# First layer's sampled attention in sixteen turns, with the coverage test in PSUM and merged value products

## The reference, cut to what matters

```python
K, V, Qp = k @ Wk.T + bk, v @ Wv.T + bv, q @ Wq.T + bq         # first layer: 16 heads of 16
loc_x = mod(ref + (Qp @ Woff.T + boff) + loc, sign_lens)       # 5 sampling points per query and head
sk, sv = 0.5 * (w0 * K[i0] + w1 * K[i1]), 0.5 * (w0 * V[i0] + w1 * V[i1])   # linear between neighbours
attn = softmax(sum_d(Qh / sqrt(16) * sk)); ctx = sum_k(attn * sv); out = ctx @ Wo.T + bo
# layers 1 to 3: dense attention; in 2 and 3 K, V have biases bk, bv, and out = ctx @ Wo + bo
```

## Time and profile before

| what | value |
|---|---|
| three runs | 1224.21, 1225.88, 1226.24 us; median 1225.88 us |
| profiled execution | 1230.04 us; its span 1228.2 us, so 1.84 us lie around the span |
| busy share of the span | PE 88%, DVE 65%, ACT 40%, POOL 18% |
| mean granted TensorE clock | 0.91 of full |
| DMA | 121.84 MB, mean 99 GB/s |

### The profile page before, as it was taken

One profiled execution on the slowest core, in us unless ns is written; L12 is line 12 of the kernel. 1 busy time (PEld: TensorE's weight loads), 2 busy tenths in 40 slices (PEclk: granted clock), 3 DMA queues, 4 the chain that ended last, 5 costly groups with the idle time before them and its releaser, 6 DMA issues.

```text
span 1228.2 us, 17469 instructions
## 1 busy us (share of the span) xinstructions
PE 1079.4 (88%) x6632; PEld 626.1 (51%) x6632; DVE 801.3 (65%) x1433; ACT 488.2 (40%) x712; POOL 221.7 (18%) x264
## 2 busy tenths in 40 slices
PE   8598994899998886998799999889789999699898
PEld 4245552344443443997344444444578787244445
DVE  4978948688978813354578886971644654689716
ACT  2453221066766650111016775664312221057552
POOL 3563811211111002000501110100400400211000
PEclk9798896789999996999869999999999999679899
DMA  5686820201331052794151231200244240100001
GB/s 187 217 250 208 296 84 1 84 21 39 122 101 38 11 156 72 263 371 157 41 162 41 60 87 50 55 6 14 91 156 151 88 149 27 29 7 16 1 27 35
DMA packets 78571, 121.84 MB, mean 99 GB/s; under 512 B 9888, under 2 KB 52036, under 8 KB 78478
## 3 DMA queue, kind: packets, MB, share of 16 engines
q1 hardware_dynamic: 58778, 79.41, 21.0%
q10 hardware_dynamic: 18932, 39.10, 9.1%
q0 software_dynamic: 768, 2.10, 0.5%
HBM read 92.45 MB, written 27.81 MB: 98 GB/s over the span
## 4 chain that ended last, share of the span: by engine, by line
PE 61%; DVE 23%; issue 4%; ACT 3%; DMA 2%; POOL 2%; ACTq 0%; SPq 0%; DVEq 0%; POOLq 0%
DVE arena L1955 13%; PE bank L1373 11%; PE bank L1333 11%; PE bank L1544 10%; PE st_bank L1472 3%; PE bank L1484 3%; PE st_bank L1358 3%; PE st_bank L1241 2%; DVE xn L1655 2%; PE st_bank L1544 2%; PE bank L1403 1%; PE st_bank L1301 1%; PE bank L1339 1%; PE bank L1182 1%; PE st_bank L1249 1%
## 5 line engine op out<-in xcount | busy, mean ns | idle before, releaser
L1955 DVE TENSOR_REDUCE arena<-bank 128x1 f32<-128x512 f32 x640 | 400.2, 683 | 70.8 <-PE bank L1333 70.7
L1056 ACT ACTIVATE arena<-st_bank 128x1024 f32<-128x1024 f32 x320 | 316.1, 1022 | 159.2 <-PE st_bank L1358 157.8
L1333 PE MATMUL bank<-g_a 64*128 64x512 f32 x480 | 184.9, 517 | 13.4 <-DVE arena L1955 3.3
L1373 PE MATMUL bank<-arena,vaug 128*9 128x256 f32 (+2 forms) x2560 | 177.0, 396 | 1.8 <-ACT arena L1056 1.8
L1333 PEld LDWEIGHTS bank<-g_a 64*128 64x128 f32 x480 | 75.7, 199 | 122.9 <-DVE arena L1955 83.8
L1544 PE MATMUL bank<-g_a,g_w 128*128 128x512 f32 x512 | 117.6, 390 | 4.3 <-DVE g_w L2157 3.2
L1358 PE MATMUL st_bank<-g_a 64*128 64x512 f32 x480 | 117.7, 445 | 0.0
L1544 PEld LDWEIGHTS bank<-g_a,g_w 128*128 128x128 f32 x512 | 95.8, 188 | 25.4 <-DVE g_w L2157 3.6
L1373 PEld LDWEIGHTS bank<-arena,vaug 128*9 128x9 f32 (+2 forms) x2560 | 56.8, 93 | 81.5 <-issue 44.4
L1333 PE MATMUL bank<-g_x,g_a 64*128 64x512 f32 x160 | 64.2, 528 | 9.9 <-DVE arena L1955 3.2
L837 POOL CAST arena<-arena 8x128 fp32r<-8x128 f32 x40 | 11.2, 280 | 315.4 <-ACT arena L1049 315.4
(11 more groups left out here) (284 smaller groups left out, 1506.0 us busy)
## 6 DMA issues: line engine op xcount, KB each, us to landing
arena<-in_glu_w SPq DMA_DIRECT2D x39, 512.0 KB, 3.3
arena<-kv_table SPq DMA_DIRECT2D x16, 1024.0 KB, 7.1
ctxT<-in_glu_w ACTq DMA_DIRECT2D x22, 512.0 KB, 6.5
arena<-in_w SPq DMA_DIRECT2D x20, 512.0 KB, 6.3
kparts<-arena ACTq DMA_DIRECT2D x12, 512.0 KB, 3.9
arena<-in_w ACTq DMA_DIRECT2D x12, 512.0 KB, 3.5
g_a<-kparts SPq DMA_DIRECT2D x24, 192.0 KB
kv_table<-arena ACTq DMA_DIRECT2D x16, 256.0 KB, 2.1
```

The source lines that it names most:

```text
L1056: act.activation(prob[sl % PROBS], st_bank[sl % 2][:], ACT.Exp, scale=scale).then_inc(exp_ready, 1)
L1333: pe.matmul(bank[TURN_BANKS[place % 3]], Qc[gi % KQ_BUFS][rows, hh, qt * P:(qt + 1) * P], Kc[gi % KQ_BUFS][rows, half * CH:(half + 1) * CH ...
L1373: ins = pe.matmul(bank[7][at:at + dh + 1, 0:D], vaug[l][:, b * KT + 2 * m + i, h0 + hh, :], tiles[:, a], start=(m == 0 and i == 0), stop=( ...
L1955: dve.tensor_reduce(mxh[gi % 2][:, col, hf:hf + 1], bank[TURN_BANKS[place % 3]], AX.X, ALU.max).then_inc(max_red, 1)
```

## The change

The two loops over tiles on DVE and POOL become one loop of 16 turns, a product each. The softmax is done by batch inside the turns: the maximum of a batch in turn 4 or 8, its subtraction, exponential and sum in the next, its scaling in the one after; the weighing by the attention of tile t stands in turn t + 6, so that turns 6 to 8 weigh for both kinds of product. POOL's product n waits for the weighing of turn n - 1. The weighing by the attention has a buffer of its own (`a_tmpv`). `rest` is called by a list (`RESTS`): none in turns 0 to 3, one each in 4 to 10, two in 11 to 13, three in 14.

The coverage test works by batch on halves of 320 elements, in PSUM banks 2 and 3, with a help array in SBUF; two tiles of the table go ahead of it. Its sum is taken by PE after ten of the sixteen table products, in bank 0, and the flag is made after turn 2. DVE then reads two flags and runs turns 3 to 15 in one of two copies, with or without the general path:

```diff
+            kv0_rows(KV_FIRST, KV_FIRST + KV_BY_DVE)
+            for b in range(B):
+                ins = dve.tensor_scalar(inside[b], points[b], float(M // 2 - BACK), float(-M), ALU.is_ge, ALU.mult)
...
+            def turn(n, uncovered):
+                if n in (QT + 1, NT + 1):
+                    b = n // NT
+                    dve.tensor_tensor(sc[:, rows_b[b]], sc[:, rows_b[b]], each_sample(a_mx, b), ALU.subtract).then_inc(sub0_ready, 1)
+                if n in (QT + 2, NT + 2):
+                    b = n // NT
+                    ch.link(dve.scalar_tensor_tensor(sc[:, rows_b[b]], sc[:, rows_b[b]], 0.5, each_sample(a_sm, b), ALU.mult, ALU.mult))
+                weighed = n - QT - 2
+                if 0 <= weighed < NT:
+                    last = weigh(weighed)
+                if 1 <= n <= NT:
+                    last = weigh_scores(n - 1)
...
+                elif 1 <= n < 2 * NT - 2:
+                    last.then_inc(prod_used, 1)
+                dve.wait_ge(prod_ready, n + 1)
...
+                if n < len(RESTS):
+                    for k in range(sum(RESTS[:n]), sum(RESTS[:n + 1])):
                         rest(k)
...
+            with dve.If(all_covered):
+                for n in range(FLAG_AT + 1, 2 * NT):
+                    turn(n, False)
...
+            with dve.If(some_uncovered):
+                for n in range(FLAG_AT + 1, 2 * NT):
+                    turn(n, True)
+                dve.wait_ge(ctxn_ready, NT)
+                general(1, range(NT), more_context)
+            dve.wait_ge(ctxn_ready, NT)
             dve.sem_inc(ctxn_ready, NT)
```

On PE the key products go round four banks, and the three value products of a chunk become one of 416 columns without bias products. ACT's three value copies now read that one bank. The value biases of layers 2 and 3 go into the output bias instead: bo + bv @ Wo, made by PE after the gate logits and copied by ACT; PE's ranking comes behind these products:

```diff
+                if k >= 4:
+                    pe.wait_ge(prepk_lo, k - 3)
...
+                for i in range(DC):
+                    ins = pe.matmul(bank[QT_BANKS[k % 4]][:, 0:VW], ctxT[:, i, k * P:(k + 1) * P], a_wv[:, i, :], start=(i == 0), stop=(i == DC - 1))
...
+            for l in (2, 3):
+                o = bank[5][0:1, (l - 2) * D:(l - 1) * D]
+                for c in range(EC[l]):
+                    pe.matmul(o, w[l]["bv"][:, c:c + 1], w[l]["o"][:, c, :], start=(c == 0), stop=False)
+                ins = pe.matmul(o, onesf[0:1, 0:1], w[l]["bo"][:], start=False, stop=True)
+            ins.then_inc(prepv_mm, 1)
             pe.wait_ge(onehot_ready, 1)
```

ACT's order changes with it: row weights 4 to 6 go between the last table copies, weights 7 behind the first chunk, and the two exponentials behind chunks 1 and 5. SP has two more small loads (the value biases) among the late ones, reads the flag ahead of all value windows, and has three skips of the general path in place of two:

```diff
-            for t in range(NWIN):
-                window_load(NT + t, t, 1)
             sp.wait_ge(flag_ready, 1)
...
+            general_windows(0, range(QT))
+            for t in range(QT):
                 window_load(NT + t, t, 1)
-            general_windows(1, NT)
+            general_windows(0, range(QT, NT))
+            for t in range(QT, NT):
+                window_load(NT + t, t, 1)
+            general_windows(1, range(NT))
```

More of the change, by code:

```diff
@@ L109 @@
 KCHUNKS = PREP0[4]
+PREP_BANKS = (2, 3, 4, 5)
+VW = sum(EW.values())
+V0 = {l: sum(EW[i] for i in range(1, l)) for l in ATT}
+RESTS = [0] * 4 + [1] * 7 + [2] * 3 + [3]
+assert sum(RESTS) == KCHUNKS
+KV_BY_DVE = 2
+FLAG_AT = 2
 QT_BANKS = (0, 1, 6, 7)
@@ L424, in build @@
         a_W = r2.take([NT, HK, WIN])
-        a_S = [r2.take([WIN, H0]) for _ in range(2)]
+        a_S = [r2.take([WIN, H0]) for _ in range(3)]
         r3 = Region(w0kv_at)
         a_A = [r3.take([H0, WIN]) for _ in range(3)]
+        a_tmpv = r3.take([HK, WIN])
+        assert r3.at <= w0q_at
         a_tmp = Region(w0q_at).take([HK, WIN])
@@ L940, in _ @@
             row_weights(1)
-            for n in range(KV_FIRST, 2 * KV_FIRST, 2):
-                kv0_store(n)
-                kv0_store(n + 1)
-                if n < 2 * KV_FIRST - 2:
-                    row_weights((n - KV_FIRST) // 2 + 2)
-            for n in range(2 * KV_FIRST, NCT):
-                kv0_copy(n)
-                if n > 2 * KV_FIRST:
-                    kv0_store(n - 1)
-            kv0_store(NCT - 1)
+            for i in range(3):
+                kv0_store(KV_FIRST + 2 * i)
+                kv0_store(KV_FIRST + 2 * i + 1)
+                if i < 2:
+                    row_weights(2 + i)
+            kv0_copy(12)
+            row_weights(4)
+            kv0_copy(13)
+            kv0_store(12)
+            kv0_copy(14)
+            kv0_store(13)
+            row_weights(5)
+            kv0_copy(15)
+            kv0_store(14)
+            row_weights(6)
+            kv0_store(15)
             act.wait_ge(ld_small, 16 * 4)
@@ L1242, in _ @@
                 ins.then_inc(prepk_mm, 1)
[L1243 to L1252 removed]
+                if k >= 4:
+                    pe.wait_ge(prepv_evac, k - 3)
@@ L1745, in rest @@
                 dve.wait_ge(prepk_hi, k + 1)
-                src, (hi, lo) = bank[2 + k % 2][0:n, :], (a_parts[k % PBUFS][0:n, i] for i in range(PARTS))
+                src, (hi, lo) = bank[PREP_BANKS[k % 4]][0:n, :], (a_parts[k % PBUFS][0:n, i] for i in range(PARTS))
                 if l == 1:
@@ new lines, in _ @@
+            kv0_rows(KV_FIRST, KV_FIRST + KV_BY_DVE)
+            for b in range(B):
+                ins = dve.tensor_scalar(inside[b], points[b], float(M // 2 - BACK), float(-M), ALU.is_ge, ALU.mult)
+            ch.link(ins)
+            for b in range(B):
+                ins = dve.scalar_tensor_tensor(points[b], points[b], float(BACK), inside[b], ALU.add, ALU.add)
+            ch.link(ins)
+            for b in range(B):
+                ins = dve.tensor_scalar(inside[b], points[b], 0.0, None, ALU.is_ge)
@@ new lines, in _ @@
+            for n in range(FLAG_AT + 1):
+                turn(n, None)
+            dve.wait_ge(sum_mm, 2)
+            dve.tensor_scalar(flag_i[:, 0:1], bank[0][0:1, 0:1], float(P * NT * HK) - 0.5, None, ALU.is_lt)
+            dve.tensor_scalar(flag_i[:, 1:2], bank[0][0:1, 0:1], float(P * NT * HK) - 0.5, None, ALU.is_ge).then_inc(flag_ready, 1)
+            dve.wait_ge(flag_ready, 1)
+            some_uncovered, all_covered = (dve.value_load(flag_i[0:1, i:i + 1], min_val=0, max_val=1) for i in range(2))
```

307 lines of the change are left out of this document (146 added, 161 removed).

## The result

The changed kernel takes 1194.55 us in the median of four runs (1193.10 to 1195.89) against 1225.05 for the kernel before beside it: ratio 0.9752, 95% interval 0.9732 to 0.9771. The profiled execution took 1195.89 us, span 1193.4, mean clock 0.914.

What follows compares the result with a forecast made beforehand. POOL's sixteen products were the longest chain, their idle time on the path through the key preparation. Transposes 23.3 us sooner, 1.5 gained, 3 and 2.2 lost: -19.6 from 1230.04, adjusted to the median, gave 1206 us, range 1196 to 1217.

Steps and rivals of the forecast that it cites:

- Start, turns 2 to 7, softmax: DVE and POOL, start to product 8: product 2 at 50.1 us (9.2 gained), product 7 at 82.5, softmax inside the turns.
- First value window: SP's late loads and skip delay the first window: it lands at 91.6 us, product 8 at 92, 3 late (0 to 6).
- Key preparation: Last four turns: turn 14 waits for stores and for PE partly at half clock, 6 us (0 to 14).
- The rival that I gave 0.18: DMA transfers take over between 74 and 137 us: windows and stores 6 to 8 us late, 1213 us; chance 0.18.
- The skip: DVE's branch over the general copy after the last value sum: 2.5 us (1 to 4) on the path.
- Behind the stage: After the transposes begin: 1.5 us gained on ACT's context copy, 3 lost to PE's half clock (0 to 6).
- The bias products: Second layer, five products between logits and ranking: 5 to 5.5 us, making the ranking 2.2 us later (0 to 3).
- The sum: Whole kernel: -23.3 - 1.5 + 3 + 2.2 = -19.6 us, predicting 1206 us.
- everything fits: Whole stage: chunks keep up, PE stays warm, first window in time, transposes at 143 or sooner, 1197 us; chance 0.15.
- the rival that ended slower: PE's key preparation at half clock takes over the stage: transposes at about 183 us, time 1242; chance 0.06.

Runs made afterwards that it cites:

- the run with the windows first: Changed kernel with SP's fifteen late loads behind all eight value windows instead of ahead of the first; ratio 0.9802 to the kernel before, stage 102.2 us.
- at the old price: Changed kernel with a key chunk's value products by layer again, eight instead of two; ratio 0.978 to the kernel before, stage 103.9 us.
- the twelve loads out of the way: Changed kernel, value windows ahead of late loads, twelve loads issued after the last sum; ratio 0.9760 to the kernel before, 0.9765 with stores also issued sooner.
- The run with the skip behind the sum: Changed kernel with DVE waiting for the last value sum inside the covered branch, before the skip; ratio 0.9785 to the kernel before, stage 104.7 us.
- the run with the test alone: Kernel before with only the new coverage test (in PSUM, by batch, its halves around the first table tiles); ratio 0.994 to the kernel before.

## Why the prediction was wrong, step by step

The forecast's times, counted from product 0 (38.92 before), beside three profiles of the changed kernel:

| us after product 0 | forecast | first | second | third |
|---|---|---|---|---|
| product 2 | 11.2 | 12.0 | 12.5 | 12.5 |
| product 5 | 28.4 | 28.7 | 28.9 | 28.9 |
| product 6 | 36.1 | 35.1 | 35.4 | 35.4 |
| product 7 | 43.6 | 42.2 | 42.5 | 42.5 |
| product 8 | 53.1 | 52.4 | 54.8 | 57.1 |
| product 11 | 72.5 | 71.0 | 72.0 | 74.1 |
| product 15 | 93.6 | 92.0 | 92.3 | 94.0 |
| last sum issued | 103.7 | 98.3 | 98.9 | 101.1 |
| transposes | 108.4 | 101.6 | 102.3 | 103.8 |

**Start, turns 2 to 7, softmax: right.** Every product up to product 15 stands within 1.6 us of its forecast in the first profile. The coverage test was priced at 0.5 an instruction and took 0.45. Its reason was half right: not PSUM alone, but also which instructions stand beside a product, and which kind they are.

**First value window: right in place, open in size.** 5.6 us of gap against "some 5" in the first profile; 10 in the third. SP's late loads set it, as the run with the windows first showed. While the window was late, the softmax by batch was worth only 0 to 2 us.

**Key preparation: the step that failed.** I put its tail at 6 us (0 to 14). Product 15's sum was issued 2.4, 2.7 and 3.2 us after the product, so the tail is 2.4 to 3.2. The mechanism was there, DVE waiting for ACT in turns 13 and 14 and ACT for stores, but I added PE at half clock to it, and PE was ahead. In the first profile its granted clock was 1.00 from 105 to 135 us, its chunk took 3.11 us, the pairs overlapping (3.43 for the last four), not 3.55, and at the old price it lengthened the stage by only 2. What the tail hangs on is the transfers. The pages' DMA issues, first of before and then of after, give the stores of 512 KB that ACT waits for 3.9 and 5.8 us to landing:

```profile
kparts<-arena ACTq DMA_DIRECT2D x12, 512.0 KB, 3.9
...
kparts<-arena ACTq DMA_DIRECT2D x12, 512.0 KB, 5.8
```

The rival that I gave 0.18 has its mechanism shown, and its sign too: four of the eight value windows landed after 9 us or more in the first profile, none before. Its price (6 to 8 us) is not shown. In the changed kernel the tail costs the 2.4 to 3.2, and with the windows sooner, the stores sooner and the twelve loads out of the way the whole stage is 4 to 6 us shorter still.

**The skip: mis-sized.** 2.5 us forecast, 0.4 to 1.1 measured. I read 2.15 and 3.05 as a price to be added; but here a skip runs from the issue of the instruction ahead of it (2.4 to 3.9 us from there in all these kernels), and a 2.27 us sum now stands there. The Trainium skill's page Runtime: NRT & Kernel Launch (Instruction fetch mechanics) says that a taken branch to a target outside the fetched pages waits until that page is fetched. The run with the skip behind the sum agrees, with 3.89 us of waiting and nothing beside it; the fetch itself no run shows.

**Behind the stage: nearly right.** I forecast 1.5 lost between the transposes and the attention behind them (3 for the clock, 1.5 gained on ACT). From the first transpose to the first attention product it took 60.3 us before and 62.3, 61.1 and 61.2 after: 0.8 to 2.0. In the two kernels in which TensorE was busy up to the transposes and kept the full clock it took 58.1 and 58.3. So some 2 us were gained there (1.5 forecast, from ACT's copy), and the half clock took back 3 to 4 (3 forecast). The bias products cost 1.1 at the ranking (DVE goes on 4.9 us after the logits, against 3.8), not 2.2: they took 4.5 us, not 5 to 5.5, and DVE's marks come 3.2 us after the logits anyway.

**The sum.** Tail and skip account for 5 of the 11.5 us, the bias products for 1.1. Product 15's place 1.6 and the earlier start 1.7 were in the first profile, but not in all; some 2 us are left to the spread of executions, which I can't assign. How large that spread is shows behind the second layer's first attention product, where I counted 2.2 us of new work: that part took 997.3 us before and 992.3, 995.9 and 992.1 after. So the fall below the range is in part luck; the tail and the skip are not. The closest case was *everything fits* (transposes at 143 or sooner, 1197). For the rival that ended slower nothing spoke: PE's preparation ended 5 us ahead of the transposes.

**What stays open**: why the half clock comes behind a busy preparation in some executions and not in others. In the run with the test alone it took back 10 us.

## What to carry to other kernels

When a wait is taken off a chain, look at what the queues carry in the last third of the stage: here the buffers of a side task, held until their stores landed, decided the end, and loads moved out of the way of one wait only came down on the next. Price a skipped branch from the issue of the instruction ahead of it, and leave a long one there. Read a stage of 100 us from landmarks in the trace, when executions differ by more than the edit.

## What the runs showed of the hardware

- DVE instructions of the form tensor_scalar with SBUF operands waited for a running POOL product (3.20 us for two, 0.88 from PSUM). So did tensor_tensor: the weighing at 90.04 of the changed kernel took 4.45 us beside product 8, 1.28 elsewhere. One scalar_tensor_tensor (0.48) and two tensor_reduce (0.88) beside product 1 did not; that product took 4.87 us instead of 4.52. The Trainium skill's page GPSIMD Engine Reference (Specifications) lists POOL's SBUF interfaces as shared with VectorE, with contention from DVE instructions in a 2-port mode or with two SBUF inputs. The tensor_tensor agrees, and the tensor_scalar fits, which between the products took 0.56 us for two from SBUF; the one scalar_tensor_tensor, which has two SBUF inputs, wasn't held.
- DVE's skip of a long branch showed 3.89 us with nothing beside it and as little as 0.42 behind a sum of 2.27; from the issue of the instruction ahead of it, the skips of these kernels took 2.4 to 3.9.
- With the preparation busy to the end, the projections ran at 0.50 (1.2 GHz) for at least 26 us, although PE was 98% busy in them; in the first profile of the changed kernel, after 5 us of idle time, the half clock was over with the first projection.
